# Adding x to three of four output quarters: VectorE after a load, or accumulating DMAs issued by GpSimd

## What is computed

```
q   = relu(cond @ W3 + b3)                       # one row of 1024 per batch
v   = (n * x + sum over tokens of x) * q         # n = 512 tokens
y   = relu(v @ W2 + b2)                          # 1024 x 1024, stage 1
gates = softmax(y @ W_router + b_router)         # 6 experts, the best 2 kept
out = x + (y @ W_base + b_base) + low-rank parts of y through A_s, B_s and the gated A_r, B_r   # stage 2
```

## Time and profile before

| | |
|---|---|
| device time, median of 3 runs | 1411.26 us (1410.85 to 1411.5) |
| span of the profiled execution, first to last instruction | 1409.3 us |
| PE (TensorE matmul) busy | 1405.1 us |
| DVE (VectorE) busy | 909.1 us |
| ACT (ScalarE) busy | 607.0 us |
| POOL (GpSimd) busy | 18.8 us |
| DMA | 200.03 MB, mean 142 GB/s |

### The profile page before, as it was taken

One profiled execution on the slowest core, in us unless ns is written; L12 is line 12 of the kernel. 1 busy time (PEld: TensorE's weight loads), 2 busy tenths in 40 slices (PEclk: granted clock), 3 DMA queues, 4 the chain that ended last, 5 costly groups with the idle time before them and its releaser, 6 DMA issues.

```text
span 1409.3 us, 18037 instructions
## 1 busy us (share of the span) xinstructions
PE 1405.1 (100%) x6177; PEld 1156.1 (82%) x6177; DVE 909.1 (65%) x1563; ACT 607.0 (43%) x1140; POOL 18.8 (1%) x65
## 2 busy tenths in 40 slices
PE   9999999999999999999999999999999999999999
PEld 6888888888888888888888888888888888888887
DVE  6977565765656656567889566655655656556564
ACT  7774645546455464645544231332312323132230
POOL 3000000000000000000000000000000000000000
PEclk9999999999999999999999999999999999999999
DMA  8242414334142342426727527163361634617242
GB/s 315 81 159 84 158 50 141 104 91 154 55 140 98 104 148 59 144 82 223 267 92 210 190 95 249 63 219 137 110 241 61 232 119 136 216 60 268 84 148 91
DMA packets 135580, 200.03 MB, mean 142 GB/s; under 512 B 38752, under 2 KB 39008, under 8 KB 135488
## 3 DMA queue, kind: packets, MB, share of 16 engines
q1 hardware_dynamic: 134624, 197.66, 42.2%
q10 hardware_dynamic: 864, 1.22, 0.2%
HBM read 127.12 MB, written 71.70 MB: 141 GB/s over the span
## 4 chain that ended last, share of the span: by engine, by line
PE 100%; DVE 0%; DVEq 0%; issue 0%
PE ps L1633 33%; PE ps L1635 33%; PE ps L1634 33%; PE ps L1644 1%; PE ps L1659 0%; PE ps L1653 0%; DVE buf L1626 0%; DVEq L57 0%; DVE zeros L1261 0%
## 5 line engine op out<-in xcount | busy, mean ns | idle before, releaser
L1633 PE MATMUL ps<-act_hi,w_hi 128*128 128x512 f32 x1792 | 697.3, 389 | 0.0
L1635 PE MATMUL ps<-act_hi,w_lo 128*128 128x512 f32 x1792 | 697.1, 389 | 0.0
L1634 PE MATMUL ps<-act_lo,w_hi 128*128 128x512 f32 x1792 | 697.1, 389 | 0.0
L1633 PEld LDWEIGHTS ps<-act_hi,w_hi 128*128 128x128 f32 x1792 | 336.3, 188 | 70.6 <-DVE act_lo L1099 0.9
L1635 PEld LDWEIGHTS ps<-act_hi,w_lo 128*128 128x128 f32 x1792 | 336.3, 188 | 69.9
L1634 PEld LDWEIGHTS ps<-act_lo,w_hi 128*128 128x128 f32 x1792 | 336.3, 188 | 69.8
L675 ACT ACTIVATE act_hi<-src 128x512 fp32r<-128x512 f32 x256 | 156.3, 625 | 256.3 <-PE ps L1635 254.6
L1163 DVE SCALAR_TENSOR_TENSOR buf<-ps,bb_sb,buf 128x512 f32<-128x512 f32 x127 | 95.0, 750 | 157.8 <-PE ps L1635 142.1
L1106 DVE TENSOR_TENSOR act_lo<-src,act_hi 128x512 fp32r<-128x512 f32 x192 | 130.3, 684 | 36.2 <-ACT act_hi L675 36.2
L1099 DVE SCALAR_TENSOR_TENSOR act_lo<-src,shift,act_hi 128x512 fp32r<-128x512 f32 x128 | 95.2, 748 | 30.4 <-ACT act_hi L672 30.4
L694 ACT ACTIVATE yhi<-buf 128x512 fp32r<-128x512 f32 x128 | 80.0, 625 | 65.2 <-PE ps L1635 65.1
(11 more groups left out here) (119 smaller groups left out, 1018.1 us busy)
## 6 DMA issues: line engine op xcount, KB each, us to landing
src<-in_xT SPq DMA_DIRECT2D x224, 256.0 KB, 2.8
y_scratch<-buf SPq DMA_DIRECT2D x128, 256.0 KB, 2.1
src<-y_scratch SPq DMA_DIRECT2D x128, 256.0 KB, 5.1
outT<-buf SPq DMA_DIRECT2D x127, 256.0 KB, 3.8
buf<-in_xT SPq DMA_DIRECT2D x32, 256.0 KB, 5.0
wl_raw<-in_wbase SPq DMA_DIRECT2D x6, 1024.0 KB, 6.0
r<-in_w SPq DMA_DIRECT2D x15, 256.0 KB, 9.7
grow<-gates_scratch SPq DMA_DIRECT2D x96, 32.0 KB, 2.1
```

What stands on the lines that cost most here:

```text
L1633: nc.tensor.matmul(out, wh, a_h, start=start, stop=False, skip_group_check=onto)
L1634: nc.tensor.matmul(out, wh, a_l, start=False, stop=False, skip_group_check=onto)
L1635: return nc.tensor.matmul(out, wl, a_h, start=False, stop=stop, skip_group_check=onto)
```

## The change

x of the quarters C11, C21 and C22 is no longer loaded into `src` and added by VectorE. GpSimd issues, for each of these tiles, a DMA that reads x from HBM and adds it onto the tile in SBUF (`accum_op=ALU.add`), 12 a pair, 96 in all. The three VectorE functions go, and with them 96 of SyncE's loads. SyncE stores a C11 tile when its accumulating DMA has landed (`x11_added[j]`). `c22` and `c21` wait for theirs (`x22_added[j]`, `x21_added[j]`). As `G12` and `G22` hold no x now, the next pair's y tiles are loaded into them at the places in SyncE's list where x was loaded before. The C12 quarter is as it was.

```diff
+            def add_x(out, b, t, added):
+                pool.dma_start(out, xT[b, t], accum_op=ALU.add).then_inc(added, 16)
+
+            for p in range(NP):
+                for j in range(H):
+                    pool.wait_ge(u2_copied, four(NP + p, j))
+                    add_x(buf2[:, j, :], 2 * p, H + j, x21_added[j])
+                    pool.wait_ge(c11_low, four(p, j))
+                    add_x(buf1[:, j, :], 2 * p, j, x11_added[j])
+                for j in range(H):
+                    pool.wait_ge(u4_copied, four(NP + p, j))
+                    add_x(buf3[:, j, :], 2 * p + 1, H + j, x22_added[j])
...
                 for k in range(H):
                     sp.wait_ge(lo_done, op_no(g, 3, k))
-                    sp.dma_start(src[:, tile(G12, k), :], xT[2 * p, k]).then_inc(x_loaded[tile(G12, k)], 16)
+                    if more:
+                        load_y(p + 1, G12, k)
...
                 for k in range(H):
                     sp.wait_ge(lo_done, op_no(g, 4, k))
-                    sp.dma_start(src[:, tile(G22, k), :], xT[2 * p, H + k]).then_inc(x_loaded[tile(G22, k)], 16)
-                for j in range(H):
-                    sp.wait_ge(c11_out, four(p, j))
+                    if more:
+                        load_y(p + 1, G22, k)
+                for j in range(H):
+                    sp.wait_ge(x11_added[j], 16 * (p + 1))
                     sp.dma_start(outT[2 * p, j], buf1[:, j, :]).then_inc(buf1_stored[j], 16)
-                    sp.dma_start(src[:, tile(G12, j), :], xT[2 * p + 1, H + j]).then_inc(x_loaded[tile(G12, j)], 16)
...
-                    for k in range(H):
-                        sp.wait_ge(x22_added, four(p, k))
-                        load_y(p + 1, G12, k)
...
-                    for k in range(H):
-                        sp.wait_ge(x21_added, four(p, k))
-                        load_y(p + 1, G22, k)
...
             def c22(g, j):
                 dve.wait_ge(u4_copied, four(g, j))
+                if g >= NP:
+                    dve.wait_ge(x22_added[j], 16 * (g - NP + 1))
...
             def c21(g, j):
                 dve.wait_ge(u2_copied, four(g, j))
+                if g >= NP:
+                    dve.wait_ge(x21_added[j], 16 * (g - NP + 1))
...
-                    c11_add_x(p, j)
...
-                    u4_add_x(p, j)
-                    u2_add_x(p, j)
...
-                        dve.wait_ge(x22_added, four(p, j - 1))
...
-                dve.wait_ge(x22_added, four(p, H - 1))
...
-                dve.wait_ge(x21_added, four(p, H - 1))
...
+            dve.wait_ge(x21_added[H - 1], 16 * NP)
             dve.wait_ge(bank_done, group_no(ALL - 1, 6, H - 1))
```

More of the change, by code:

```diff
@@ L238, in adaln_ffn @@
         hw_stored = [sem("hwb_stored"), sem("hwa_stored")]
-        wl_loaded = [sem(f"wl_loaded{n}") for n in range(NPROD)]
-        wh_loaded = [sem(f"wh_loaded{n}") for n in range(NPROD)]
+        wl_loaded = {n: sem(f"wl_loaded{n}") for n in (0, 1, 2, 4, 5, 6)}
+        wh_loaded = {n: sem(f"wh_loaded{n}") for n in (2, 5)}
         wb_s1 = sem("wb_s1")
@@ L258, in adaln_ffn @@
         c11_low = sem("c11_low")
-        c11_out = sem("c11_out")
         x12_loaded = [sem(f"x12_loaded{j}") for j in range(H)]
-        x22_added = sem("x22_added")
-        x21_added = sem("x21_added")
+        x11_added = [sem(f"x11_added{j}") for j in range(H)]
+        x22_added = [sem(f"x22_added{j}") for j in range(H)]
+        x21_added = [sem(f"x21_added{j}") for j in range(H)]
         last_half_stored = sem("last_half_stored")
@@ L291, in gate_no, with loads @@
             return 2 * i + w + 1
[L293 to L297, removed]
+        def loads(g):
+            return 16 * (g + 1)
         tile = lambda q, k: H * q + k
@@ L666, in high @@
                 else:
-                    act.wait_ge(x_loaded[t], loads(g, q))
+                    act.wait_ge(x_loaded[t], loads(g))
                     func = ACT.Copy if n == 0 else ACT.Relu
@@ L1119, in t1 @@
                 else:
-                    dve.wait_ge(x_loaded[t], loads(g, G12))
-                    dve.wait_ge(x_loaded[a], loads(g, G11))
+                    dve.wait_ge(x_loaded[t], loads(g))
+                    dve.wait_ge(x_loaded[a], loads(g))
                     nc.vector.tensor_tensor(src[:, t, :], src[:, t, :], src[:, a, :], ALU.subtract
@@ L1137, in t2 @@
                 else:
-                    dve.wait_ge(x_loaded[tile(G22, k)], loads(g, G22))
+                    dve.wait_ge(x_loaded[tile(G22, k)], loads(g))
                     nc.vector.scalar_tensor_tensor(buf3[:, k, :], src[:, tile(G22, k), :], 0.0,
@@ L1508, in c11_add_low @@
                                         ALU.add).then_inc(c11_low, 1)
[L1510 to L1514, removed]
             def c12_out(p, j):
@@ L1519, in c12_out @@
                 add_bank(j, bb_sb[:, j:j + 1], buf1[:, j, :], c12_done)
[L1521 to L1531, removed]
             def pair2(p):
```

## The result

The changed kernel takes 1416.04 us (median of 6 runs, 1413.82 to 1417.51) against 1411.33 us (median of 6, 1410.58 to 1411.98). The ratio is 1.0034 with a 95% interval of 1.0023 to 1.0046: 4.7 us slower, past the bound of 2.8 us that the prediction set for "same". The span of the profiled execution grew from 1409.3 to 1414.3 us; its device time of 1416.13 us lies 1.8 us above it, and in every other run with both on record, of either kernel, the two lie 1.7 to 1.9 us apart. So nothing was lost outside the span.

The account below looks back on a forecast made before the run. TensorE's matmuls were taken to bound the kernel, untouched by the change: 1409.3 - 0 + 0 = 1409.3 us profiled. With the median 2.0 us above that, the forecast was 1411.3 us, range 1410.0 to 1414.5.

Parts of the forecast that it names:

- same: The verdict of no change, for a measured time within 0.2%, 2.8 us; given chance 0.85.
- What bounds the kernel: In stage 2 TensorE never waits, 443 matmuls per 100 us; any gain is bounded by its 4.2 us idle.
- The C11 path of pairs 1 to 7: From C11's added x through its store and the C12 loads to `c12_out`, priced in pair 3: TensorE stalls 0.
- the choice of values: For C11's accumulating DMAs: issue at most 1.19 us, landing 5.6 us taken, between bounds of 2.8 and 13.4.
- Before SyncE is even there: In pair 3, C11's fourth tile has its x by 1012.8, before SyncE can start the stores at 1014.2.
- Only C11 feeds back to TensorE: In stage 2, of the changed quarters only C11 can make TensorE wait; deadline for its fourth tile 1024.3.
- No queue fills: Twelve accumulating DMAs a pair add 9.5 us in 87 us, or 0.11 to a DMA share of at most 0.50.
- What is moved: The next pair's eight y tiles, loaded where x was, cost 0: some 50 us of cover against a 5.1 us landing.
- DMAs that run one behind the other: Rival: accumulating DMAs land in 5.0 us each without overlap, TensorE waits at every product 5, 1506 us; chance 0.07.
- a GpSimd held off by VectorE: Rival: none of the eight DMAs starts before VectorE's chain ends at 1007.2; 23 us in 8 pairs, 1434 us; chance 0.04.
- a fixed price: Rival: a third DMA queue costs time outside the chain, 1413.3 us, or about 1415 if over 2.8 us; chance 0.02.

Follow-up runs that it names:

- hold_x21: The changed kernel, but in pair 0 the four accumulating DMAs of C21 are issued only after the low-rank operand hb has landed; 1412.67 us, ratio 1.0014.
- clear0: The changed kernel with, in pair 0, C21's accumulating DMAs issued after hb landed and the next pair's eight y tiles after the second grow loads; 1411.19 us, ratio 1.0002.
- gates_first: The changed kernel with pair 0's six loads of the gate weights issued right behind the store they read, ahead of two y tiles; 1415.98 us, ratio 1.0031.
- traffic: The kernel before the change plus eight plain HBM-to-HBM copies of x tiles, results unused, issued by GpSimd in pair 0; 1414.36 us, ratio 1.0022.
- late_c11: The changed kernel, but in pairs 1 to 7 C11's four accumulating DMAs are issued only after the last copy of C22; 1471.56 us, ratio 1.0425.

## Why the prediction was wrong

- **What bounds the kernel** held. TensorE does the same 443 matmuls in 100 us wherever it doesn't wait, and 57.9 us less of VectorE gave nothing.
- **The C11 path of pairs 1 to 7** held, and with it the choice of values. GpSimd issued in 0.87 us each (0.856 to 1.213, the slowest a hair over the upper bound of 1.19). The landing was 6.1 us at the median (3.9 to 8.9), for 5.6 taken and 13.4 as the upper bound. In pair 3, where all is 4.9 us later than before, the first load of x for C12 is issued at 1024.55, which is 1019.6 in the old times, just as in the earlier trace rows:

```profile
1019.52 2.75 SPq L535 DMA_DIRECT2D outT<-buf  x4
1024.55 4.10 SPq L538 DMA_DIRECT2D buf<-in_xT  x4
1032.01 0.75 DVE L1168 SCALAR_TENSOR_TENSOR buf<-ps,bb_sb,buf 128x512 f32<-128x512 f32 x1 [7.37 <-DMA buf<-in_xT]
1035.80 0.75 DVE L1168 SCALAR_TENSOR_TENSOR buf<-ps,bb_sb,buf 128x512 f32<-128x512 f32 x1 [0.52 <-PE ps L1621]
```

  But those loads land after 7.1 us at the median of the four, for 5.2 before, and `c12_out(0)` ends 3.0 us ahead of TensorE, for 5.2 before. The prediction had no term for what the new traffic does to the transfers beside it.
- **"Before SyncE is even there"** did not hold. The sum let the eighth DMA start at 1007.2, with no limit on how many are in flight. In pair 3 it starts at 1014.36 and lands at 1021.92, which is 1009.5 and 1017.0 in the old times: 4.2 us later than the 1012.8 taken, still inside the 1020.6. The fourth C11 store waits for it, in five of the eight pairs:

```profile
SPq L535 <- DMA buf<-in_xT: 3.0, 5, 0.9
```

  Nothing came of it, as the first load of x for C12 needs only the first store. So that this path cost 0 was right, with less room than the text claims.
- **The step that failed** is the sentence "Only C11 feeds back to TensorE". It was drawn from pair 3 and taken for all eight pairs. Pair 0 has a second way to TensorE, whose calls stand in the code under `if p == 0`: the gates of the last pair of stage 1, through a store, six loads, a store and a load. It had 0.4 us to spare. No row of pair 0 was read, though the answer was one window away.
- **"No queue fills"** failed with it. The bandwidth was averaged over a pair: 0.11 more on a share of at most 0.50. The doubled cost of a tile was sized right (1.55 us, for 2 x 0.79), and the windows of 100 us show the rise that was worked out (0.41 to 0.53 after, between 800 and 900). But eight of the twelve fall in some 17 us, where the share passes 1.
- **What is moved** was costed by whether its own reader waits. That was right (nobody waits for the y tiles), but in pair 0 they are in others' way: with the C21 DMAs held they cost some 1.2 us, as hold_x21 lies 1.6 us over the kernel before and clear0 0.3 us.
- **The rivals** named DMAs that run one behind the other, a GpSimd held off by VectorE, and a fixed price. None came as priced. The first came in part: three run at a time, and the eight of pair 3 are issued 1.85 us apart on average ((1014.36 - 1001.44) / 7), where the rival put the limit at 3.5 us. The rule of the Trainium skill ("SBUF — State Buffer", section "SBUF: two separate sides") that GpSimd is locked out while VectorE holds the shared ports shows in no issue here: the longest of 96 is 1.213 us, beside two-input instructions of VectorE (that section's warning names its two-port modes). That agrees with the same page's "Who interferes with whom". Nor are GpSimd's pauses VectorE's doing: in the one of 1.39 us ahead of 749.33 VectorE is idle itself, waiting for the grow loads. The slower case that did come, contention with a way that has no slack, had no chance of its own, so 1.3 in 10 for slower was too little and the range ended 1.5 us too low.

## What to carry to other kernels

Where a loop's first or last turn has calls of its own, read that turn for slack too; a steady turn says nothing of them. When a change moves bytes earlier or makes them dearer, list every DMA-fed wait in the same 20 us, with its slack, not only the readers of the moved data, and take the DMA share in windows of 5 us there. The cure was order, not fewer bytes: transfers that nobody waits for go behind the short chain that somebody does. And count how many transfers an issuer has in flight before adding up its issues: a limit there moves every later one.

## What the runs showed of the hardware

An accumulating DMA of a 256 KB tile takes 1.55 us of all 16 DMA engines and 144 packets; the same one without the addition takes 0.88 us and 80. It lands after 6.1 us at the median, 3.8 without the addition.

In all eight profiled executions with accumulating DMAs GpSimd issues none while three are in flight (3 x 144 packets). Without the addition up to six are (6 x 80 packets). Whether packets set the limit or something else, no run here shows.

TensorE's clock did not fall after every wait of the same length. After the 2.94 us in the changed kernel its PEclk is 0.68 in the window from 760 to 765; in gates_first, after 2.89 us, it stays 1.00:

```profile
760.00:765.00 5.00, 2.52 (x11) 1.00 1.03 266
```

The runs of the changed kernel differ by the same sign: the fastest, 1413.82 us, has a mean clock of 1.000 and the other five 0.999. The traces have one more difference. In the changed kernel a wait of 0.35 us, at 758.10, comes 3 matmuls ahead of the long one, and traffic (2.77, then 0.30 us; PEclk 0.69) and pair 0 of late_c11 (0.42, then 2.64 us; PEclk 0.74) have such a pair too, while the 2.89 us of gates_first stand alone. Whether that decides it, these runs do not show.
